# Placing the edges of a graph layer by matmuls with masks, and two equal chunks of edges

## The chip, the core and the metric

One core of a Trainium2 chip runs the kernel. Its engines are TensorE (PE, with its weight loads as PEld), VectorE (DVE), ScalarE (ACT), GpSimd (POOL) and SyncE (SP), each with its own stream of instructions, coupled by semaphores. The metric is the device time of one execution in microseconds; lower is better.

## What is computed

```python
xn = layernorm(x)                       # x: 6250 x 256
agg = segment_sum(xn[nbr], dst_of_edge) # 100000 edges
mean = agg / max(count, 1)
x = x + xn @ W1.T + b1 + mean @ W2.T + b2 + mix(xn)   # mix: 8 heads of key-value products, plus xn
x = x + experts(layernorm(x))           # top-1 of 8 experts, capacity 977
```

The edges' source ids aren't sorted by the node they are summed into, so the kernel sorts them itself. It brings every edge into a slot of a "tile" of 128 slots, in which all edges belong to one block of 128 nodes (49 blocks).

## The kernel before

Five stages follow one another.

**1. Table, counts and places of chunk 0.** The edges lie as 125 partitions by 800 columns, and two chunks of columns are sorted apart: 352 columns and then 448 (`chunk_plan`, L51). For the layernorm and the table of `xn` times W2 in two float16 parts, eight blocks at a time go through VectorE (`pair`, L753), ScalarE (`normal`, `turned`, `high`), TensorE (`turn`, `table`, L515 to L536) and out by GpSimd's queue. Between these, VectorE finds each edge's place. `count` (L879) makes a mask of "edge is of block b" for each of 49 blocks and counts it by an accumulator; `place` (L815 on VectorE, L546 on TensorE) turns the counts into the place where each block begins on each partition; and `rank` (L898) makes the mask again, runs a prefix sum over it (the scan, L911) and copies the sums under the mask into `pos` (L918). One turn of the loop at L921 is `rank` for 7 blocks and then one `pair`.

**2. Sort of chunk 0.** For each column of edges VectorE writes one-hots of the slot in its tile (`LH`, L945; every third column a scaled one too, L952) and of the tile (`HT`, L956). ScalarE scales them (`LV`, L479), and two matmuls (L566) add the edge's two numbers into banks `psV`. `decode` (L863) makes `idx` and `srcl` of them. The gathers wait for it.

**3. Tiles of chunk 0.** GpSimd issues one indirect gather of 128 rows per tile (L398) into a ring of 32; TensorE multiplies it with a one-hot of its nodes (L586, L587); VectorE adds the result to the block (L804). Between tiles, VectorE does all of `second_chunk` (L962), that is counts, places and sort of chunk 1, split over the tiles by `side_plan` (L85), which has a cost for each step and must be done 32 tiles before the chunk's end; `columns_by` tells TensorE which columns to multiply behind which tile.

**4. Tiles of chunk 1.** Between the tiles the head products (`heads`, one per group of 16 tiles) and then each block's own product with W1 (`own`, one block per 4 tiles, L636 on TensorE and L1091 on VectorE).

**5. Nodes and experts** (`nodes`, `experts`), which the change doesn't touch.

Chunk 0 has 400 tiles (`T0`), chunk 1 has 496: the count is an upper bound on what any graph needs, rounded up to 16. The tiles that no edge fills gather one and the same row 128 times.

Of the kernel before, what the change touches and what calls it, by code (L numbers as in the profile page):

```python
# [5 lines left out]
ALU = mybir.AluOpType  # L6
# [10 lines left out]
P = 128  # L17
# [62 lines left out]
HEAD0, KV_AT = 1, 1 + NB // HD + 1  # L80
OWN0 = KV_AT
assert len(CHUNKS) == 2 and OWN0 + NB // LD + 1 <= CHUNKS[1][3] // GR and NB % LD == 1 and COLS1 % LB == 0


def side_plan():  # L85
# [16 lines left out]
    return done, place, sort, decode  # L102


SIDE, PLACE, SORT, DECODE = side_plan()
PLACE_AT = next(t for t in range(T0) if SIDE[t] > PLACE)
DECODE_AT = next(t for t in range(T0) if SIDE[t] > DECODE)

# [95 lines left out]
def edges(nc, ctx, kk, dram, x, src, dst, w1t, w2t, gb1, gb2, kw, kb, vw, vb, gate_w, gate_b):  # L204
# [5 lines left out]
    def sem(name):  # L210
# [26 lines left out]
    b7 = sb("b7", [P, B7], F32)  # L237
    n7 = sb("n7", [P, B7], F32)
# [21 lines left out]
    cnt = sb("cnt", [P, NB], F32)  # L260
    mi = sb("mi", [P, 2 * NB], I32)
    mrow = sb("mrow", [P, NB], F32)
    mend = sb("mend", [P, NB], F32)
    base = sb("base", [P, NB], F32)
# [34 lines left out]
    s_cnt, s_pre, s_mc, s_ec, s_ge, s_bk = (sem(n) for n in (  # L299
        "bucket_counts", "bucket_prefix", "tile_counts", "tile_ends", "tiles_past_ends", "tile_buckets"))  # L300
# [21 lines left out]
    block = ctx.enter_context(nc.Block())  # L322

# [183 lines left out]
    def _(pe):  # L507
# [30 lines left out]
        def table_of(i):  # L538

            turn(4 * i, 8 * i, 2)  # L540
            for g in range(4 * i, 4 * i + 4):
                if g < 4 * i + 3:
                    turn(g + 1, 2 * g + 2, 2)
                table(g, 2)

        def place(c, pp, pq):  # L546
            tiles = CHUNKS[c][3]
            pe.wait_ge(s_cnt, c + 1)

# [44 lines left out]
        table_of(0)  # L594
        place(0, psP, psQ)
        n = NB // (2 * LD)
        for i in range(1, n):
            table_of(i)
# [56 lines left out]
        for t in range(T0, TILES):  # L655
            g, s = (t - T0) // GR, (t - T0) % GR
            if g == KV_AT and s == 0:
# [11 lines left out]
            if HEAD0 <= g < KV_AT and s >= 10:  # L669
                m, pieces = g - HEAD0, (HD if g - HEAD0 < NB // HD else 1) * 2  # L670
                if s == 10:
                    pe.wait_ge(s_kn, m + 1)
                products(m, range(min(s - 10, pieces), min(s - 9, pieces)), pieces - 1)
            if OWN0 <= g and s % 2 == 0 and (g - OWN0) * LD + s // 4 < NB:
                own((g - OWN0) * LD + s // 4, s % 4)

    @block.vector
    def _(v):
# [17 lines left out]
        v.tensor_copy(iota_b[:, :], iota_i[:, 0:NB])  # L696
        v.tensor_copy(XA[:, RW - 1:NB * RW:RW], mi[:, 0:NB])
# [852 lines left out]
```

## Time and profile before

| what | us |
|---|---|
| median of 3 runs (2236.62 to 2239.11) | 2238.36 |
| the profiled execution | 2236.5 |
| its span | 2234.9 |

| engine | busy us | share |
|---|---|---|
| PE | 1573.9 | 70% |
| DVE | 1518.3 | 68% |
| POOL | 1056.0 | 47% |
| ACT | 721.1 | 32% |

A share over the whole span mixes five stages with different limits, so it tells little here. The stages are to be read apart, from the busy times of stretches and from the moments at which the work of one stage lets the next begin. In a row of the timeline, the first number is the start, the second the duration; the bracket at the end tells how long the engine sat idle before and what it waited for. PEclk is the granted TensorE clock, as a share of 2.4 GHz.

### The profile page before, as it was taken

To read this page: it belongs to the slowest core of one execution; us is meant where nothing else is said; L and a number is where in the kernel's file an instruction comes from. 1 tells how busy PE (TensorE), PEld (TensorE's weight loads), DVE (VectorE), ACT (ScalarE), POOL (GpSimd) and SP (SyncE) were. 2 spreads that over 40 slices of the span, in tenths; PEclk is the share of its full clock that TensorE was granted. 3 is DMA by queue.
4 is the path that set the end of the run, shared out by engine and by line. 5 is a ranking of instruction groups with operands and counts; after the bars stand their busy time and mean duration, and the time that the engine had idled before them with its cause. 6 is when DMAs were issued, how large, how long until landed. Compare 5 with 4: busy or idle time off the path is not lost. (4 is left out here: it accounts for less than half of the span.)

```text
span 2234.9 us, 27232 instructions
## 1 busy us (share of the span) xinstructions
PE 1573.9 (70%) x6303; PEld 838.9 (38%) x6303; DVE 1518.3 (68%) x4295; ACT 721.1 (32%) x2020; POOL 1056.0 (47%) x1037
## 2 busy tenths in 40 slices
PE   2363887444477777766565557888747499999997
PEld 2351332110022222223222224444436266666665
DVE  8978999899988888877665656555457144444444
ACT  1243998000077777720000001111036122222221
POOL 2001000777777766667777777777705311111111
PEclk8677999555599999975555556766555599999999
DMA  4117000333333322463333334444745512222310
GB/s 141 38 57 299 12 0 0 97 92 90 90 99 104 97 81 78 79 99 98 104 106 101 103 104 130 127 126 121 94 110 202 163 48 87 94 92 95 96 49 5
DMA packets 89940, 212.70 MB, mean 95 GB/s; under 512 B 20882, under 2 KB 50104, under 8 KB 86848
## 3 DMA queue, kind: packets, MB, share of 16 engines
q0 software_dynamic: 52656, 140.17, 23.9%
q1 hardware_dynamic: 35496, 70.56, 9.4%
q8 instruction: 50, 0.82, 0.2%
q10 hardware_dynamic: 1680, 0.67, 0.1%
q14 instruction: 58, 0.48, 0.1%
HBM read 166.08 MB, written 49.89 MB: 97 GB/s over the span
## 5 line engine op out<-in xcount | busy, mean ns | idle before, releaser
L398 POOL DMA_INDIRECT G<-xn_parts,idx x448 | 455.0, 1016 | 339.6 <-DVE srcl L876 165.1
L804 DVE TENSOR_TENSOR XA<-XA,bank 128x257 f32 x896 | 375.3, 419 | 333.6 <-PE bank L587 302.0
L479 ACT ACTIVATE LV<-LH,v 125x128 f16<-125x128 f16 x1490 | 449.5, 387 | 340.4 <-DVE LH L1003 309.3
L398 POOL DMA_INDIRECT w<-xn_parts,idx x448 | 459.2, 1025 | 136.5 <-issue 136.5
L566 PE MATMUL bank<-HT,LV 125*128 125x496 f16 (+1 forms) x1600 | 401.4, 359 | 141.9 <-ACT LV L479 66.8
L586 PE MATMUL bank<-G,S 128*128 128x257 f16 x448 | 159.1, 355 | 199.2 <-DMA G<-xn_parts,idx 166.5
L1520 POOL DMA_INDIRECT out<-ob,tok x64 | 66.7, 1042 | 402.3 <-DVE ob L1506 399.6
L586 PE MATMUL bank<-w,S 128*128 128x257 f16 x448 | 158.8, 355 | 135.1 <-DMA w<-xn_parts,idx 118.7
L566 PEld LDWEIGHTS bank<-HT,LV 125*128 125x128 f16 x1600 | 117.6, 98 | 361.4 <-ACT LV L479 187.1
L1444 PE MATMUL bank<-w,ht 128*117 128x256 f32 (+1 forms) x1024 | 223.7, 379 | 0.0
L1433 PE MATMUL bank<-xt,w 128*128 128x468 f32 (+1 forms) x512 | 215.6, 580 | 0.8 <-ACT xt L1458 0.8
L1444 PEld LDWEIGHTS bank<-w,ht 128*117 128x117 f32 (+1 forms) x1024 | 188.8, 186 | 30.5 <-issue 0.4
L1468 ACT ACTIVATE ht<-bank,b1c 128x468 f32<-128x468 f32 (+1 forms) x128 | 85.7, 669 | 334.1 <-PE bank L1433 334.1
L1497 DVE TENSOR_TENSOR y<-bank,b 128x256 f32<-128x256 f32 (+1 forms) x64 | 27.2, 424 | 235.2 <-PE bank L1444 235.2
L586 PEld LDWEIGHTS bank<-G,S 128*128 128x128 f16 x448 | 47.3, 106 | 330.0 <-DMA G<-xn_parts,idx 270.4
L587 PE MATMUL bank<-G,S 128*128 128x256 f16 x448 | 164.8, 368 | 0.0
L587 PE MATMUL bank<-w,S 128*128 128x256 f16 x448 | 164.3, 367 | 0.0
L586 PEld LDWEIGHTS bank<-w,S 128*128 128x128 f16 x448 | 47.0, 105 | 274.7 <-DMA w<-xn_parts,idx 220.5
L1008 DVE TENSOR_SCALAR HT<-iota_t,tf 125x496 f16<-125x496 f16 x448 | 149.5, 362 | 0.0
L1433 PEld LDWEIGHTS bank<-xt,w 128*128 128x128 f32 x512 | 98.1, 192 | 109.6 <-issue 107.1
L784 DVE TENSOR_TENSOR S<-iota,srcl 128x1024 f16<-128x1024 f16 x112 | 136.6, 1220 | 2.3 <-issue 2.2
L489 ACT ACTIVATE work<-work 128x768 f32<-128x768 f32 (+1 forms) x17 | 13.9, 818 | 315.8 <-DVE work L1039 315.8
(223 smaller groups left out, 2073.9 us busy)
## 6 DMA issues: line engine op xcount, KB each, us to landing
w<-f SPq DMA_DIRECT2D x16, 1024.0 KB, 7.4
expert_rows<-G SPq DMA_DIRECT2D x7, 2048.0 KB, 19.4
xb<-expert_rows SPq DMA_DIRECT2D x8, 1028.0 KB, 11.9
xb<-expert_rows SPq DMA_DIRECT2D x8, 939.7 KB
G<-xn_parts,idx POOLq DMA_INDIRECT x448, 2.8
w<-xn_parts,idx POOLq DMA_INDIRECT x448, 2.8
XA<-x SPq DMA_DIRECT2D x6, 1024.0 KB, 5.6
xn_parts<-G POOLq DMA_DIRECT2D x12, 512.0 KB, 3.7
```

What stands on the lines that cost most here:

```text
L398: pool.indirect_dma_start(g[:, o:o + 2 * D], None, tab, bass.IndirectOffsetOnAxis(ap=idx[:, t:t + 1], axis=0)).then_inc(s_g[t % RING], 16)
L479: ins = act.activation(LV[0:EP, (2 * q + n) * P:(2 * q + n + 1) * P], LH[0:EP, q * P:(q + 1) * P], ACT.Copy, scale=v[0:EP, ds(col, 1)])
L566: ins = pe.matmul(psV[n][:, 0:tiles], LV[0:EP, (2 * q + n) * P:(2 * q + n + 1) * P], HT[0:EP, q * TMAX:q * TMAX + tiles], start=False, sto ...
L586: pe.matmul(psA[t % AR][:, 0:AGW], lhs, g[:, o + D:o + 2 * D + 1], start=True, stop=True)
L587: pe.matmul(psA[t % AR][:, 0:D], lhs, g[:, o:o + D], start=False, stop=True, skip_group_check=True).then_inc(s_tile, 1)
L784: v.tensor_tensor(S[:, t % SR * P:(t % SR + SB) * P].rearrange("p (j n) -> p j n", n=P), iota_1[:, :].unsqueeze(1).to_broadcast([P, SB, P] ...
L804: v.tensor_tensor(XA[:, ds(o, AGW)], XA[:, ds(o, AGW)], psA[t % AR][:, 0:AGW], ALU.add).then_inc(s_ev, 1)
L1008: v.tensor_scalar(HT[0:EP, (q + j) * TMAX:(q + j) * TMAX + tiles], iota_t[0:EP, 0:tiles], tf[0:EP, k + j:k + j + 1], None, ALU.is_equal).t ...
L1433: ins = pe.matmul(psH[f % 2][:, 0:cols], w1[q][:, k * F + f * P:k * F + (f + 1) * P], xt[n % 2][:, k * TQ * P:k * TQ * P + cols], start=(k ...
L1444: ins = pe.matmul(psY[m % 2][0:rp, 0:D], ht[:, f * TQ * P + m * rp:f * TQ * P + (m + 1) * rp], w2[q][:, f * D:(f + 1) * D], start=(f == 0) ...
L1468: act.activation(ht[:, f * TQ * P:f * TQ * P + cols], psH[f % 2][:, 0:cols], ACT.Relu, bias=b1c[:, e * FT + f:e * FT + f + 1]).then_inc(s_ ...
L1520: pool.indirect_dma_start(out, bass.IndirectOffsetOnAxis(ap=tok[0:rp, s:s + 1], axis=0), ob[0:rp, s * D:(s + 1) * D], None, bounds_check=N ...
```

## The change

- Chunks of 400 and 400 columns; tiles are rounded up to 8, so 440 and 440 (880 in all instead of 896).
- `count` goes: VectorE only makes the mask (L888 of the changed kernel, no accumulator). TensorE multiplies each mask with a one-hot pattern `to_row` (L576), which adds, in one bank, the number of edges of block b in every column, in row b and once more in row 64 + b.
- `place` makes one scan over the 400 columns of that bank (L895 of the changed kernel) and from it the places at which each column of each block begins, as two bfloat16 parts in `begin16`.
- `rank` has no scan: two matmuls per block, mask times a triangle (`before`) and `of_row` times `begin16` (L597, L598), give the places in a bank, and VectorE copies them under the mask (L935). In chunk 0 two banks take turns (`psP`, `psQ`), in chunk 1 four.
- Chunk 0's counts are 25 and 24 behind the first two `pair`s, its ranks 12, 12, 12 and 13 behind the other four, and TensorE does them between its table matmuls. The loops are written out.
- In stage 3 the planner has lower costs for counts and ranks. In stage 4 a head product takes 12 tiles (`HS`) and a block's own product 3 (`OS`).

```diff
-    for cols in (352, 448):
+    for cols in (400, 400):
         tiles = (cols * EP + NB * (P - 1)) // P
-        tiles = -(-tiles // GR) * GR
+        tiles = -(-tiles // SB) * SB
...
+HS, OS = 12, 3
+HEAD0 = GR
+KV_AT = HEAD0 + HS * (NB // HD + 1)
...
+COUNTS = (25, 24)
+RANKS = (12, 12, 12, 13)
...
-    split = rank + NB + 2
+    split = rank + NB + RB1
-    costs = [800] * NB + [9000] + [2300] * (NB + 2) + [700] * 5 + ([1070] + [350] * (LB - 1)) * (COLS1 // LB) + [3000]
+    costs = [430] * NB + [8000] + [1100] * (NB + RB1) + [700] * 5 + ([1070] + [350] * (LB - 1)) * (COLS1 // LB) + [3000]
...
+        def counted(c, b, pp):
+            cols = CHUNKS[c][1]
+            m = 2 * c * NB + b
+            pe.wait_ge(s_mk, m + 1)
+            pe.matmul(pp[0:SROWS, 0:cols], to_row[0:EP, NB - 1 - b:NB - 1 - b + SROWS], masked(c, m), start=(b == 0),
+                      stop=(b == NB - 1)).then_inc(s_mu, 1)
...
+        def ranked(c, b, ring):
+            cols = CHUNKS[c][1]
+            m = (2 * c + 1) * NB + b
...
+            pe.wait_ge(s_mk, m + 1)
+            if b >= len(ring):
+                pe.wait_ge(s_cp, c * NB + b - len(ring) + 1)
+            out = ring[b % len(ring)][0:EP, 0:cols]
+            pe.matmul(out, before[0:EP, 0:EP], masked(c, m), start=True, stop=False)
+            pe.matmul(out, of_row[0:SROWS, b:b + 1].to_broadcast([SROWS, EP]), begin16[0:SROWS, 0:cols],
+                      start=False, stop=True).then_inc(s_mu, 1)
...
+        def mask_of(c, m, b):
+            c0, cols = CHUNKS[c][0:2]
+            if m >= B7:
+                v.wait_ge(s_mu, m - B7 + 1)
+            v.tensor_scalar(masked(c, m), blk[0:EP, c0:c0 + cols], iota_b[0:EP, b:b + 1], None,
+                            ALU.is_equal).then_inc(s_mk, 1)
...
+        def rank(c, r, ring):
...
+                mask_of(c, m, r)
+            if r >= n:
+                b = r - n
+                v.wait_ge(s_mu, m - n + 1)
+                if b:
+                    v.wait_ge(s_cp, c * NB + b)
+                v.copy_predicated(pos[0:EP, 0:cols], masked(c, m - n).bitcast(U16),
+                                  ring[b % n][0:EP, 0:cols]).then_inc(s_cp, 1)
...
-        with v.Fori(0, NB // B7) as i:
-            step_count.loop(i, 3)
-            count(i)
...
+        for i in range(PAIRS):
+            if i:
+                pair(i, True)
+            if i < len(COUNTS):
+                for b in range(sum(COUNTS[:i]), sum(COUNTS[:i + 1])):
+                    mask_of(0, b, b)
...
+                    place(0, psP, psQ)
+            else:
+                j = i - len(COUNTS)
+                for r in range(sum(RANKS[:j]), sum(RANKS[:j + 1])):
+                    rank(0, r, (psP, psQ))
```

How this moves instructions at two places:

TensorE, table phase, one group of eight blocks before (L524 transposes the normalized rows, L534 multiplies them with W2):

```order
L524 MATMUL bank<-ident,XA 128x128 x8
L534 MATMUL bank<-W,LV 128x256 x4
L524 MATMUL bank<-ident,XA 128x128 x4
L534 MATMUL bank<-W,LV 128x256 x4
L524 MATMUL bank<-ident,XA 128x128 x4
L534 MATMUL bank<-W,LV 128x256 x8
```

The begin of such a group after the change, in the part with ranks (L547 and L557 are the old L524 and L534):

```order
L547 MATMUL bank<-ident,XA 128x128 x4
L597 MATMUL bank<-mask,before 125x400
L598 MATMUL bank<-cum,of_row 125x400
L597 MATMUL bank<-mask,before 125x400
L598 MATMUL bank<-cum,of_row 125x400
L547 MATMUL bank<-ident,XA 128x128 x4
L557 MATMUL bank<-W,LV 128x256 x4
```

Two or three ranks have come between every two table products, so each is held up by masks and copies of VectorE, and the copies by the table.

TensorE, tiles of chunk 1, the blocks' own products before (L643 transposes, L649 and L651 multiply with W1 and add the bias, L586 and L587 are a tile):

```order
L643 MATMUL bank<-ident,work 128x128 x2
L586 MATMUL bank<-w,S 128x257
L587 MATMUL bank<-w,S 128x256
L586 MATMUL bank<-G,S 128x257
L587 MATMUL bank<-G,S 128x256
L649 MATMUL bank<-W,work 128x256 x2
L651 MATMUL bank<-brow,ones 128x256
```

And after the change (L703, L709, L711 and L628, L629 are the same lines):

```order
L703 MATMUL bank<-ident,work 128x128 x2
L628 MATMUL bank<-w,S 128x257
L629 MATMUL bank<-w,S 128x256
L709 MATMUL bank<-W,work 128x256 x2
L711 MATMUL bank<-brow,ones 128x256
```

One tile instead of two lies between a block's transposes and its products, and three instead of four between one block and the next.

## Rows read from the trace of the kernel before

**Rows 1.** Busy time by stretches: microseconds, and in brackets instructions, of each engine.
```profile
core 0: us, PE busy (x) PEld busy (x) DVE busy (x) ACT busy (x) POOL busy (x), PEclk, DMA share, GB/s
70.00:204.00 134.00, 60.75 (x248) 49.22 (x248) 110.84 (x281) 48.11 (x94) 13.46 (x15) 0.70 0.27 103
204.00:391.00 187.00, 150.40 (x706) 55.55 (x706) 178.25 (x889) 175.94 (x594) 0.17 (x1) 0.98 0.11 47
391.00:442.00 51.00, 21.70 (x72) 4.80 (x72) 47.41 (x137) 0.00 (x0) 39.13 (x38) 0.51 0.33 95
470.00:611.00 141.00, 57.88 (x192) 12.70 (x192) 132.19 (x248) 0.00 (x0) 111.75 (x97) 0.50 0.31 90
650.00:750.00 100.00, 77.47 (x371) 28.91 (x370) 85.49 (x225) 76.47 (x252) 76.23 (x79) 1.00 0.36 103
800.00:900.00 100.00, 77.83 (x376) 29.35 (x375) 84.02 (x224) 76.98 (x253) 62.39 (x60) 1.00 0.28 80
1000.00:1300.00 300.00, 178.84 (x668) 80.67 (x668) 192.35 (x387) 15.98 (x30) 229.30 (x233) 0.52 0.36 102
1400.00:1500.00 100.00, 84.16 (x315) 47.47 (x313) 55.16 (x127) 13.24 (x39) 76.23 (x79) 0.72 0.44 129
1590.00:1617.00 27.00, 19.61 (x60) 10.16 (x58) 11.81 (x26) 2.45 (x7) 20.30 (x23) 0.50 0.90 84
```

**Rows 2.** Timeline: GpSimd's first gathers of both chunks, last gather, last tile's add.
```profile
391.59 1.03 POOL L398 DMA_INDIRECT G<-xn_parts,idx  x1 [164.13 <-DVE srcl L876]
...
974.93 0.95 POOL L398 DMA_INDIRECT G<-xn_parts,idx  x1 [0.96 <-DVE srcl L876]
...
1616.83 0.95 POOL L398 DMA_INDIRECT w<-xn_parts,idx  x1 [0.30 <-issue]
...
1637.10 0.42 DVE L804 TENSOR_TENSOR XA<-XA,bank 128x257 f32 x1 [0.20 <-DVE XA L804]
```

**Rows 3.** Groups by line: name, count, then busy us and mean ns of one.
```profile
L911 DVE TENSOR_TENSOR_SCAN cum<-onesw,n,mask 125x352 f32<-125x352 bf16 x49 | 45.4, 938 | 0.2
...
L918 DVE COPY_PREDICATED pos<-mask,cum 125x352 f32<-125x352 uint16 x49 | 26.0, 531 | 1.0
...
L956 DVE TENSOR_SCALAR HT<-iota_t,here 125x400 f16<-125x400 f16 x352 | 96.4, 314 | 0.0
...
L1008 DVE TENSOR_SCALAR HT<-iota_t,tf 125x496 f16<-125x496 f16 x448 | 149.5, 362 | 0.0
```

**Rows 4.** Timeline, one group of eight blocks in the table phase, and the next one's begin.
```profile
103.77 1.97 PE L524 MATMUL bank<-ident,XA 128*128 128x128 f32 x8 [6.22 <-ACT XA L424]
...
111.84 3.62 PE L534 MATMUL bank<-W,LV 128*128 128x256 f32 x16
...
113.65 1.40 DVE L722 BATCH_NORM_STATS2 lnst<-XA 128x6 f32 x4
...
122.44 1.97 PE L524 MATMUL bank<-ident,XA 128*128 128x128 f32 x8 [6.98 <-ACT XA L424]
```

**Rows 5.** Timeline, VectorE: counts' begin and end, first ranks, and the last step before the sort.
```profile
28.94 0.17 DVE L880 COPY b<-iota_b 125x7 f32 x1
...
59.60 0.06 DVE L811 MEMSET mcol<- 128x4 f32 x1
...
65.34 1.64 DVE L904 TENSOR_SCALAR mask<-blk,b 125x352 bf16<-125x352 bf16 x7
...
204.38 0.34 DVE L859 CAST pos<-cum 125x352 f32<-125x352 int32 x1
```

**Rows 6.** Timeline, VectorE: two turns of the sort loop over 16 columns.
```profile
303.59 0.17 DVE L936 COPY here<-pos 125x16 f32 x1
...
311.77 0.17 DVE L936 COPY here<-pos 125x16 f32 x1
```

**Rows 7.** Timeline, tile stage: one gather on GpSimd, one mask on VectorE.
```profile
600.62 0.95 POOL L398 DMA_INDIRECT w<-xn_parts,idx  x1 [0.30 <-issue]
600.95 0.33 DVE L987 TENSOR_SCALAR mask<-blk,iota_b 125x448 bf16<-125x448 bf16 x1
```

More of the change, by code:

```diff
@@ L101, in side_plan, with side_by @@
     assert done[-1] == len(costs)
-    return done, place, sort, decode
-SIDE, PLACE, SORT, DECODE = side_plan()
+    assert all(b - a < RB1 for a, b in zip(done, done[1:]) if rank <= a < split)
+    return done, place, rank, sort, decode
+SIDE, PLACE, RANK, SORT, DECODE = side_plan()
 PLACE_AT = next(t for t in range(T0) if SIDE[t] > PLACE)
 DECODE_AT = next(t for t in range(T0) if SIDE[t] > DECODE)
+def side_by(t, first, n):
+    return n if t >= T0 else min(max(SIDE[t] - first, 0), n) if t >= 0 else 0
 def columns_by(t):
@@ L259, in edges @@
     tli = cum[:, WMAX:2 * WMAX].bitcast(I32)
[L260 to L264, printed above, removed]
+    mi = sb("mi", [P, NB], I32)
+    to_row = sb("to_row", [P, SROWS + NB - 1], BF16)
+    of_row = sb("of_row", [P, NB], BF16)
+    before = sb("before", [P, P], BF16)
+    ends = sb("ends", [P, SROWS], F16)
+    mc16 = sb("mc16", [P, 2], F16)
+    begins = cum[:, 0:WMAX]
+    summed = cum[:, WMAX:2 * WMAX]
+    begin16 = cum[:, 2 * WMAX:2 * WMAX + WMAX // 2].bitcast(BF16)
     mcol = sb("mcol", [P, 4], F32)
@@ L593, in _, with first_chunk @@
         ins.then_inc(s_w2n, 1)
[L594 to L598, printed above, removed]
+        def first_chunk(i, part):
+            if i < len(COUNTS):
+                b0, n = sum(COUNTS[:i]), COUNTS[i]
+                for b in range(b0 + n * part // 4, b0 + n * min(part + 1, 4) // 4):
+                    counted(0, b, psP)
+                if i == len(COUNTS) - 1 and part == 4:
+                    place(0, psQ)
+            else:
+                b0, n = sum(RANKS[:i - len(COUNTS)]), RANKS[i - len(COUNTS)]
+                for b in range(b0 + n * part // 5, b0 + n * (part + 1) // 5):
+                    ranked(0, b, (psP, psQ))
+        n = PAIRS
+        for i in range(n):
+            table_of(i, lambda part: first_chunk(i, part))
         turn(4 * n, NB - 1, 1)
@@ L696, in _ @@
         v.tensor_copy(iota_b[:, :], iota_i[:, 0:NB])
+        v.tensor_copy(before[:, :], upper[:, :])
+        v.tensor_copy(of_row[0:64, :], ident[0:64, 0:NB])
+        v.tensor_copy(of_row[64:SROWS, :], ident[64:SROWS, 64:SROWS])
+        v.tensor_copy(ends[0:NB, 0:64], upinc[0:NB, 0:64])
+        v.tensor_copy(ends[0:NB, 64:SROWS], upinc[0:NB, 0:NB])
+        step(v.memset(to_row[:, :], 0.0))
+        wait()
+        v.memset(to_row[:, NB - 1:NB], 1.0)
+        v.memset(to_row[:, 64 + NB - 1:64 + NB], 1.0)
         v.tensor_copy(XA[:, RW - 1:NB * RW:RW], mi[:, 0:NB])
@@ L840, in place @@
+            wait()
+            v.tensor_tensor(begin16[64:R, 0:cols], begins[64:R, 0:cols], begin16[64:R, 0:cols],
+                            ALU.subtract).then_inc(s_bg, 1)
             v.wait_ge(s_bk, c + 1)
@@ L877, in decode @@
             v.wait_ge(s_dec, c + 1)
-        def count(i):
-            step(v.tensor_copy(b7[0:EP, :], iota_b[0:EP, ds(i * B7, B7)]))
-            wait()
-            for j in range(B7):
-                o = j * WMAX
-                ins = v.tensor_scalar(mask[0:EP, o:o + COLS0], blk[0:EP, 0:COLS0], b7[0:EP, j:j + 1], 0.0,
-                                      ALU.is_equal, ALU.add, accum_out=n7[0:EP, j:j + 1])
-            step(ins)
-            wait()
-            step(v.tensor_copy(cnt[0:EP, ds(i * B7, B7)], n7[0:EP, :]))
@@ L926, in _ @@
+        for r in range(NB, NB + RB0):
+            rank(0, r, (psP, psQ))
         last()
-        with v.Fori(0, NB // B7 - first) as i:
-            step_count.loop(i, 2 + 2 * B7)
-            rank(i + first)
-        step_count.end(NB // B7 - first)
+        v.wait_ge(s_cp, NB)
         for _ in split(COLS0, pos):
```

186 lines of the change are left out of this document (76 added, 110 removed).

## Prediction

> **What bounds the kernel now.** I read the stretches first [rows 1], since the shares over the whole span mix five stages. Table and places (70 to 204): VectorE busy 110.84 of 134 us, TensorE 60.75. Sort of chunk 0 (204 to 391): VectorE 178.25 and ScalarE 175.94 of 187, and meanwhile GpSimd waits 164.13 us for the sorted indices [rows 2]. Tiles of chunk 0: up to 611 GpSimd issues gathers without a pause (a gather's mean is 111.75 / 97 = 1.15 us, and 0.30 us lie between two, as the last gather's bracket shows [rows 2]); from 611 on VectorE's sort of chunk 1 sets the pace, since 800 to 900 holds only 60 gathers where 650 to 750 held 79, the ring of 32 being full by then. Tiles of chunk 1: GpSimd again, 233 gathers of 0.98 us in 300 us, so 1.29 us per tile, while VectorE is busy 64% and TensorE 60%. The moments [rows 2] give the lengths: 391.59 to 974.93 is 583.3 us for 400 tiles (1.458 each), 974.93 to 1616.83 is 641.9 us for 495 steps (1.297 each), and the last tile is added 20.3 us after the last gather. This lag is read in 1590 to 1617: DMA share 0.90 at 84 GB/s, against 0.36 at 102 GB/s from 1000 to 1300. Those are the tiles that no edge fills, which read one row over and over.
>
> So the sum has five terms. Nodes and experts have the same instructions before and after: nothing.
>
> **Term 1, table and places.** Removed on VectorE: 49 scans (45.4 us) and the accumulating form of the count. The copies stay (26.0 us for 352 columns [rows 3], about 29 for 400). Removing some 65 us of work is not a gain of 65, as TensorE now stands between mask and copy, in its own order with the table. The chain per group of eight blocks is what counts. Today TensorE takes from 103.77 to 115.46, 11.7 us, and from VectorE's statistics (113.65) to TensorE's next transposes (122.44) it is 8.8 us [rows 4]. After the change both lie on one chain: VectorE can leave a group only after TensorE's tenth of 12 ranks (two banks), and that comes behind the last table product. A matmul of 400 columns costs 150.40 / 706 = 0.21 us at PEclk 0.98 [rows 1], so a rank is 0.43 us there and at most 0.85 at the half clock. A group with ranks: 8.8 + 11.7 + 10 x 0.43 = 25 us, at most 29 with the half clock; with hand-overs I take 26, against 18.7 today (103.77 to 122.44) with its ranks inside VectorE.
> Laid out: masks begin at 28.94 [rows 5]. Group 0 with 25 counts: 11.7 us and 25 x 0.21 to 0.43, ends near 48; the next normalization takes 5 of the 8.8 us, as the statistics are done by then; group 1 ends near 73. `place` took 5.7 us (59.60 to 65.34 [rows 5]) and gets two or three operations over 400 columns: VectorE is free at 79, TensorE starts group 2 at 88, group 5 at 88 + 3 x 26 = 166, and is through at 183; two last copies, the last block and five small steps make 10. The sort starts at about 193 instead of 204.4: **-12 us**. Bounds: -22 (groups of 25 and counts at full clock, 3 us less overlap loss) and +5 (groups of 29).
>
> **Term 2, sort of chunk 0.** 16 columns take 8.18 us [rows 6]. Columns go from 352 to 400, and `HT` from 400 to 440 wide. From 400 to 496 wide its mean rose from 314 to 362 ns at most [rows 3], partly by the neighbours, so 40 more are 10 to 20 ns: 8.18 + 16 x 0.01 = 8.35 us. 25 x 8.35 - 22 x 8.18 = **+29 us** (up to +32).
>
> **Term 3, tiles of chunk 0.** 440 instead of 400, and chunk 1's side work falls: no scans (49 over 448 columns, each above the 0.94 us of 352 columns [rows 3]), 400 columns for 448, and they spread over 283 tiles instead of 213, 1.41 columns per tile for 2.10. Today a tile with 2.10 columns takes 100 / 60 = 1.67 us. Taking 0.5 us for VectorE's part without columns leaves 0.55 per column, so 1.41 columns make 1.28 us. GpSimd's pace is 76.23 / 79 + 0.30 = 1.26 (650 to 750) or 1.29 (1000 to 1300): the stage becomes one of gathers. The ring lets VectorE fall back 32 tiles, so it may take (283 x 1.30 + 32 x 1.30) / 283 = 1.45 us per tile free of charge. What is issued: 38 tiles with counts at 39.13 / 38 + 0.30 = 1.33; 83 with ranks between 1.28 and today's 1.45, I take 1.38; 319 at 1.30. Sum 51 + 114 + 415 = 580 us against 583.3: **-3 us**, with bounds -14 (all at 1.29 after the counts) and +25.
> Gather and VectorE: one gather of 0.95 us, as short as they get, has a mask of 0.33 us inside it [rows 7], so I charge masks nothing. The Trainium skill (SBUF — State Buffer, "Who interferes with whom") states that `tensor_scalar` shuts GpSimd out when it runs in a two-port mode, but not in the form that writes an accumulator; that speaks against this change, which turns 49 counts from the latter form into the former. By that rule stage 3 would get up to 49 x 0.33 = 16 us longer (an estimate by that page). The row doesn't agree.
>
> **Term 4, tiles of chunk 1.** 440 x 1.297 = 571 against 641.9: **-71 us**. This is the term that carries the sum. It is hidden nowhere: the gathers follow one another here. It needs the consumers to keep up with blocks every 3 tiles. TensorE: 178.84 / 233 = 0.77 us per tile at PEclk 0.52, 84.16 / 79 = 1.07 with blocks at 0.72. Brought to 0.72 the tile is 0.56, so a block is 4 x (1.07 - 0.56) = 2.0, and with 3 tiles per block 0.56 + 0.67 = 1.23 us per tile, just under 1.30. Bounds: -74 and -45 (rival B).
>
> **Term 5, the lag at the end.** Unfilled tiles: edges fill on average 400 x 125 / 128 + 49 / 2 = 415 of 440, so 25 instead of 496 - 462 = 34. The lag of 20.3 us is 5 of ordinary lag and 15 gathered over these: 15 x 25 / 34 = 11. **-4 us**. The same 25 in chunk 0 arrive late too, but into a full ring, with nothing to be delayed but tiles that catch up.
>
> **Sum.** -12 + 29 - 3 - 71 - 4 = -61. The profiled execution took 2236.5 us (span 2234.9), 1.9 under the median of 2238.36. 2236.5 - 61 = 2175.5, beside the median 2177. I forecast **2176 us**.
>
> **Rivals.**
> *A. TensorE and VectorE wait for each other in the table phase.* Only two banks are in turn, and a table product stops the copies. If each of the four parts of a group loses 1.5 us, a group takes 32 instead of 26: 4 x 6 = +24, **2200**. For it: PEclk is 0.70 there, so the half clock is often granted. Against: more matmuls fall into the gaps in which it waits for ScalarE today. 15%.
> *B. The blocks' own products don't keep up.* With PEclk 0.52 a block is 2.8 us, a tile then 0.77 + 0.93 = 1.70; over 147 tiles 59 us fall behind, 41 are in the ring, and the rest costs about 20: **2196**. Against: 73 tiles without blocks follow, and a busier TensorE has had a higher clock (0.72 at 84% busy, 0.52 at 60% [rows 1]). 8%.
> *C. Gathers get quicker where the scans go, and the groups take 25 or less.* 83 x 0.09 + 319 x 0.02 = 14, and 8 in term 1: **2154**. 11%.
> *D. The gathers of stage 3 stay at 1.45 throughout*, because copies and onehots on VectorE stand in GpSimd's way and the split brings nothing there: 440 x 1.45 = 638, +58: **2234**, no change. 3%.
> *E. Slower: in the tiles with columns TensorE drops to the half clock.* Today it is 1.00 there at 78% busy, 77.83 / 60 = 1.30 us per tile. With 1.41 columns, 440 wide: a tile alone 0.39 (half of 0.77), a column (1.30 - 0.39) / 2.10 = 0.43, times 0.89 for the width, so 0.39 + 1.41 x 0.38 = 0.93 of 1.30 us, 72% busy, but at the half clock 1.86 us per tile. 283 x 1.86 = 526 for 368, less 42 of the ring: +116, **2292**. It is slower than today from 1.66 us per tile on. For it: in the stretch with 60% busy the clock was 0.52. Against: 72% lies nearer to 78, and at the half clock it would be busy all the time, where rows 1 shows the higher clock with more work. 5%. The Trainium skill (TensorE: Matmul & The Clock Gate, Part 1) states that the slow clock is the default and activity lifts it. By that rule E heals itself; the trace agrees as far as the busier stretches have the higher clock.
>
> **Chances and range.** Forecast 58%, A 15, B 8, C 11, D 3, E 5. The range 2145 to 2208 holds the forecast's own bounds (mainly terms 1 and 3), A, B and C, and leaves out D, E and the ends where two of the costs meet. A measurement tells about 0.2% (4.5 us) from no change. Faster 0.93, same 0.02 (D at its middle), slower 0.05 (E).
>
> **What would show it.** First gather at 405 to 412 instead of 391.59 (terms 1 and 2: sort begins near 193, 8.35 us per 16 columns). First gather of chunk 1 some 580 us later, waiting for a sort that is long done rather than for TensorE's ring. GpSimd without waits but 0.30 from there to its last gather 571 us later. PEclk near 1 in the tiles with columns and above 0.72 in those with own blocks. The forecast is wrong if stretches of stage 3 or 4 hold fewer than 75 gathers per 100 us, or if the sort starts after 205.

## The result, and the profile of the changed kernel

The change takes **2170.66 us** (median of 4 runs, 2167.32 to 2174.5) against 2238.74 for the kernel before (4 runs of the same comparison): ratio 0.9697 with an interval of 0.9675 to 0.972, so 68 us less. The forecast was 2176 us, 61 less, with a range of 2145 to 2208. The sign, the time and the range held. Of the five terms the first lay outside its bounds, the second half a microsecond over its upper one, and the prediction's view of TensorE's clock in stage 4 was wrong. The profiled execution took 2167.32 us (span 2165.4).

Stretches of the changed kernel, columns as in [rows 1]:

```profile
core 0: us, PE busy (x) PEld busy (x) DVE busy (x) ACT busy (x) POOL busy (x), PEclk, DMA share, GB/s
70.00:176.00 106.00, 64.22 (x298) 50.29 (x298) 66.59 (x198) 40.09 (x75) 8.10 (x11) 0.81 0.15 51
176.00:395.00 219.00, 179.31 (x802) 63.09 (x802) 209.15 (x1007) 200.03 (x675) 3.83 (x3) 0.98 0.18 74
400.00:500.00 100.00, 71.01 (x252) 31.43 (x251) 73.13 (x192) 0.00 (x0) 76.23 (x79) 0.60 0.36 103
650.00:750.00 100.00, 65.12 (x354) 29.26 (x354) 80.50 (x213) 63.66 (x210) 77.44 (x75) 0.98 0.35 98
800.00:900.00 100.00, 64.45 (x348) 29.12 (x349) 79.61 (x211) 61.43 (x202) 77.34 (x75) 0.98 0.34 98
1000.00:1300.00 300.00, 173.66 (x709) 87.55 (x708) 196.02 (x413) 21.53 (x45) 230.50 (x229) 0.60 0.36 103
```

The first row shows what the change took from VectorE: 66.59 us where it had 110.84 in 134 [rows 1]. The rows 650 to 750 and 800 to 900 are alike now, 75 gathers each, where there were 79 and 60: the stage has no part left in which VectorE sets the pace.

The moments, in the timeline (they answer to [rows 2, 4, 5]):

```profile
29.72 0.32 DVE L888 TENSOR_SCALAR mask<-blk,iota_b 125x400 bf16<-125x400 bf16 x1
...
62.35 0.99 DVE L895 TENSOR_TENSOR_SCAN cum<-onesw,bank 113x400 f32<-113x400 bf16 x1 [2.76 <-PE bank L576]
...
67.15 1.41 DVE L794 BATCH_NORM_STATS2 lnst<-XA 128x6 f32<-128x256 f32 x4
...
100.08 1.11 PE L547 MATMUL bank<-ident,XA 128*128 128x128 f32 x4 [8.01 <-ACT XA L447]
...
114.81 0.60 DVE L935 COPY_PREDICATED pos<-mask,bank 125x400 f32<-125x400 uint16 x1 [0.89 <-PE bank L598]
115.31 1.39 DVE L794 BATCH_NORM_STATS2 lnst<-XA 128x6 f32<-128x256 f32 x4
...
124.09 1.11 PE L547 MATMUL bank<-ident,XA 128*128 128x128 f32 x4 [8.01 <-ACT XA L447]
...
176.01 0.17 DVE L996 COPY here<-pos 125x16 f32 x1 [0.32 <-DVE pos L952]
176.14 3.53 DVE L997 COPY here<-v 125x16 f32 x1
...
395.05 1.03 POOL L421 DMA_INDIRECT G<-xn_parts,idx  x1 [173.25 <-DVE srcl L969]
...
981.59 0.94 POOL L421 DMA_INDIRECT G<-xn_parts,idx  x1 [0.30 <-issue]
...
1555.62 0.95 POOL L421 DMA_INDIRECT w<-xn_parts,idx  x1 [0.30 <-issue]
...
1569.49 0.42 DVE L877 TENSOR_TENSOR XA<-XA,bank 128x257 f32 x1 [0.85 <-PE bank L629]
```

Subtract them stage by stage. A row "tiles" is the time from the chunk's first gather to the next chunk's first, or to the last gather.

| us | before | change | difference | forecast |
|---|---|---|---|---|
| up to the sort of chunk 0 | 205.05 | 176.01 | -29.0 | -12 |
| sort of chunk 0 | 186.5 | 219.0 | +32.5 | +29 |
| tiles of chunk 0 | 583.3 | 586.5 | +3.2 | -3 |
| tiles of chunk 1 | 641.9 | 574.0 | -67.9 | -71 |
| last gather to last tile | 20.3 | 13.9 | -6.4 | -4 |
| nodes and experts, to the end | 597.8 | 595.9 | -1.9 | 0 |
| span | 2234.9 | 2165.4 | -69.5 | -61 |

The largest gain stands in stage 4, and the longer sort of chunk 0 takes half of it back. A table of differences between two kernels does not yet say which part of the change earned it: the change moves columns from the one chunk to the other, and it makes places cheaper in both. The experiments take these apart.

### The profile page after: what moved, and what is told of

Its sections match the earlier page's. It is cut to its first block and busy times, and to the rows that moved or that the text cites. A ratio compares the mean times of both kernels' runs of the same rounds, so it can differ in the third digit from the quotient of the medians.

```text
span 2165.4 us, 27487 instructions
## 1 busy us (share of the span) xinstructions
PE 1564.5 (72%) x6551; PEld 872.1 (40%) x6551; DVE 1393.2 (64%) x4116; ACT 717.9 (33%) x2005; POOL 1035.4 (48%) x1021
## 5 line engine op out<-in xcount | busy, mean ns | idle before, releaser
L877 DVE TENSOR_TENSOR XA<-XA,bank 128x257 f32 x880 | 369.3, 420 | 367.4 <-PE bank L629 344.0
L421 POOL DMA_INDIRECT G<-xn_parts,idx x440 | 445.7, 1013 | 307.1 <-DVE srcl L969 173.2
L608 PE MATMUL bank<-HT,LV 125*128 125x440 f16 x1600 | 385.0, 357 | 177.8 <-ACT LV L502 98.5
L421 POOL DMA_INDIRECT w<-xn_parts,idx x440 | 447.9, 1018 | 134.1 <-issue 134.1
L628 PE MATMUL bank<-G,S 128*128 128x257 f16 x440 | 149.5, 340 | 133.2 <-DMA G<-xn_parts,idx 104.9
L628 PE MATMUL bank<-w,S 128*128 128x257 f16 x440 | 149.9, 341 | 99.7 <-DMA w<-xn_parts,idx 88.7
L629 PE MATMUL bank<-w,S 128*128 128x256 f16 x440 | 152.8, 347 | 0.0
L629 PE MATMUL bank<-G,S 128*128 128x256 f16 x440 | 152.3, 346 | 0.0
L628 PEld LDWEIGHTS bank<-G,S 128*128 128x128 f16 x440 | 47.4, 108 | 234.8 <-DMA G<-xn_parts,idx 164.4
L1045 DVE TENSOR_SCALAR HT<-iota_t,tf 125x440 f16<-125x440 f16 x400 | 130.2, 348 | 0.0
L628 PEld LDWEIGHTS bank<-w,S 128*128 128x128 f16 x440 | 47.8, 109 | 198.1 <-DMA w<-xn_parts,idx 154.7
L1016 DVE TENSOR_SCALAR HT<-iota_t,here 125x440 f16<-125x440 f16 x400 | 114.2, 327 | 0.0
```

The source lines that it names most:

```text
L421: pool.indirect_dma_start(g[:, o:o + 2 * D], None, tab, bass.IndirectOffsetOnAxis(ap=idx[:, t:t + 1], axis=0)).then_inc(s_g[t % RING], 16)
L608: ins = pe.matmul(psV[n][:, 0:tiles], LV[0:EP, (2 * q + n) * P:(2 * q + n + 1) * P], HT[0:EP, q * TMAX:q * TMAX + tiles], start=False, sto ...
L628: pe.matmul(psA[t % AR][:, 0:AGW], lhs, g[:, o + D:o + 2 * D + 1], start=True, stop=True)
L629: pe.matmul(psA[t % AR][:, 0:D], lhs, g[:, o:o + D], start=False, stop=True, skip_group_check=True).then_inc(s_tile, 1)
L877: v.tensor_tensor(XA[:, ds(o, AGW)], XA[:, ds(o, AGW)], psA[t % AR][:, 0:AGW], ALU.add).then_inc(s_ev, 1)
L1016: v.tensor_scalar(HT[0:EP, q * TMAX:q * TMAX + tiles], iota_t[0:EP, 0:tiles], tfh[0:EP, n:n + 1], None, ALU.is_equal).then_inc(s_ht, 1)
```

## The experiments

Twelve kernels were timed, four on each of three chips, each four beside the kernel before; one kernel is among them twice. The first of the second four is the change itself, unaltered: 0.970 was expected of it on a chip like that of the result, and it came to 0.9721. Beside the first result its profile also tells what the same kernel varies by: 3.5 us in the tiles of chunk 1 (577.5 and 574.0) and 1.9 us in the lag at the end (12.0 and 13.9). The same moments of the second and third four, all in us:

| kernel | sort begins | first gather | first of chunk 1 | last gather | last tile | median | ratio (95%) |
|---|---|---|---|---|---|---|---|
| change again | 176.4 | 395.4 | 981.7 | 1559.2 | 1571.2 | 2170.1 | 0.9721 (0.9705 to 0.9737) |
| ranks alone | 192.7 | 408.9 | 996.6 | 1578.1 | 1590.2 | 2183.57 | 0.9777 (0.9761 to 0.9793) |
| spread | 179.8 | 399.9 | 986.3 | 1557.1 | 1560.7 | 2160.09 | 0.9673 (0.9657 to 0.9689) |
| 336 and 464, spread | 173.6 | 354.9 | 886.2 | 1542.4 | 1545.9 | 2146.58 | 0.9618 (0.9602 to 0.9634) |
| 368 and 432, spread | 177.1 | 377.7 | 927.2 | 1541.2 | 1544.8 | 2141.12 | 0.9592 (0.9574 to 0.961) |
| masks accumulate | 180.3 | 399.0 | 985.8 | 1561.7 | 1573.8 | 2169.1 | 0.9715 (0.9696 to 0.9735) |
| own 72 later | 177.8 | 397.7 | 981.9 | 1555.3 | 1576.1 | 2170.78 | 0.9717 (0.9697 to 0.9738) |
| even split, scans | 215.6 | 431.5 | 1033.2 | 1611.6 | 1623.1 | 2221.15 | 0.9952 (0.9935 to 0.9968) |

The kernel before took 2231.55 us (7 runs) beside the second four (the first four rows), 2232.6 (7 runs) beside the third.

### The first four: a chip on which every kernel is slower

Four kernels: the change with 352 and 448 columns, with 336 and 464, and with a block's own product every 4 tiles; and the kernel before with the even split.

```diff
-    for cols in (400, 400):
+    for cols in (352, 448):
```


> The change with its first chunk back at 352 columns and the second at 448 (392 and 488 tiles, 880 in all as in the change). Theory 'gathers set both tile stages': the unhidden sort falls by 3 x 16 columns at 8.6 us, -27 us with the narrower masks; 392 tiles at 1.33 us make 522 (586 in the change), 488 at 1.31 make 638 (574 in the change): these two cancel, total about 2141 us. Rival 'the even split pays': 448 columns at the 0.80 us of the kernel before are 358 us behind some 110 tiles of counts and ranks, the sort of chunk 1 sets the pace of stage 3, which takes 560 us or more, and the total is 2170 or above.

```diff
-    for cols in (400, 400):
+    for cols in (336, 464):
```


> The same with 336 and 464 columns (376 and 504 tiles). Gathers set the pace: another -9 us against the run with 352, about 2132. If 464 columns over 249 tiles (1.86 per tile) are more than the ring can hide (0.5 + 1.86 x 0.55 = 1.52 us per tile against 1.33 + 0.17 of the ring), it gives back 5 to 15 us and equals the run with 352; then 352 is the optimum.

```diff
-HS, OS = 12, 3
+HS, OS = 12, 4
```


> The change with a block's own product every 4 tiles again instead of 3, nothing else. Theory 'the backlog is hidden by the ring and by the tiles behind it': VectorE's lag behind the gathers stays below 10 us where the change shows 23, and the time is the same within 5 us. Rival 'TensorE at half clock delays the stage': 5 to 20 us faster. Should the profile show PEclk 0.50 with TensorE over 95% busy here too, the clock doesn't follow the load in this stage.

To the kernel before:
```diff
-    for cols in (352, 448):
+    for cols in (400, 400):
...
-        tiles = -(-tiles // GR) * GR
+        tiles = -(-tiles // SB) * SB
...
+HS, OS = 12, 3
+HEAD0 = GR
+KV_AT = HEAD0 + HS * (NB // HD + 1)
```


> The kernel before with the even split (400 and 400 columns, 440 and 440 tiles) and the 12 and 3 tile steps of stage 4, but places by VectorE's scans as before. Theory: sort +32, stage 4 -68, end -6, stage 1 +6 (49 scans and copies over 400 columns); stage 3 has 440 tiles with VectorE's scans, between 583 (400 columns instead of 448 pay for 40 tiles) and 640 (gathers at 1.45): total 2200 to 2260, I take 2215. So places by TensorE would be worth about 45 of the 68 us. Rival 'the split makes the gain': 2185 or less.

(The second of them also makes the buffer `cum` 5 * WMAX // 2 columns wide instead of 3 * WMAX.) Measured, against 2371.03 us for the kernel before on this chip (13 runs), in this order: 2322.62 (ratio 0.9786, 0.9751 to 0.982), 2307.87 (0.9748, 0.9718 to 0.9777), 2339.9 (0.987, 0.9847 to 0.9893) and 2375.31 (1.0028, 1.001 to 1.0045). The kernel before is 132 to 139 us slower here than in the other comparisons. In the third kernel, from 1100 to 1200, some waits (what waited for what: us in total, times, longest) are

```profile
PEld bank L628 <- issue: 73.5, 46, 6.2
...
DVE XA L877 <- remote: 29.3, 8, 8.4
```

and in the changed kernel, on the chip of the result, TensorE's weight loads of that line wait for landing gathers:

```profile
PEld bank L628 <- DMA G<-xn_parts,idx: 36.4, 32, 1.8
...
PEld bank L628 <- DMA w<-xn_parts,idx: 33.4, 31, 1.9
```

TensorE and VectorE stand still for up to 6 and 8 us with nothing that the profile shows to wait for. Stops of 3.3 to 9.4 us each between 413 and 462 put the tiles from 8 to 46 us behind their gathers, which fills the ring, and a tile costs 1.50 us on average in the third kernel ((1719.3 - 397.6) / 879, by its first and last gather). What stops the engines stayed open; the other comparisons don't show it. So these four tell nothing on the gathers' pace, and what the third was to tell of the half clock (blocks every 4 tiles) isn't told. They do show that the first gather moves by the sort, 397.6, 364.9 and 354.9 us for 400, 352 and 336 columns, and that the even split without the rest is no gain. The first is also the only run of the masks with the old split: 48 us less than the kernel before, on this chip. The fourth was run again on another chip.

### What the split alone brings

> The kernel before with the columns divided evenly, tiles rounded to 8 and the shorter steps of stage 4 only: VectorE keeps its accumulating counts and its scans. On the first chip of the experiments it was no faster than before (1.0028), but there all tiles took 1.5 us. Theory (the split pays only because the scans left stage 3): first gather 391.6 + 39 = 431 as on that chip; stage 3 has room for the scans only partly: 440 tiles at 1.29 to 1.47 (before had 1.458), about 615; stage 4 571; lag 14; in all some 6 us under before, ratio 0.997, while the change has 0.970 to 0.972. Rival (the split alone carries the gain of stage 4, as the prediction's largest term has it, and stage 3 does not care): stage 3 takes 586 as in the change: ratio 0.985.

The same kernel as the fourth above. **Measured 0.9952: 11 us, of the 61 that the change has in such a comparison.** The rival (0.985) falls, and the direction of the theory stands; stage 3 took 601.7 us, not 615. Its first gathers of both chunks and its last:

```profile
431.47 1.03 POOL L400 DMA_INDIRECT G<-xn_parts,idx  x1 [195.71 <-DVE srcl L882]
...
1033.18 0.94 POOL L400 DMA_INDIRECT G<-xn_parts,idx  x1 [1.25 <-PE bank L589]
...
1611.57 0.95 POOL L400 DMA_INDIRECT w<-xn_parts,idx  x1 [0.30 <-issue]
```

Against the kernel before: first gather +39.9, stage 3 +18.4, stage 4 -63.5, lag -8.7, end -1.4, together -15 of the profiled spans (which come from two chips). The split moves work, and nearly all that stage 4 wins is paid back in the places, the sort and stage 3. Against this kernel the change has its first gather 36 us earlier, and stage 3 is 15 us shorter (586.3, change again): this is what the masks on TensorE bring, with the planner's costs that go with them. The largest term of the forecast was the right number in the right stage, but it was not what made the change pay.

### Ranks within the groups, or alone

```diff
-            else:
-                b0, n = sum(RANKS[:i - len(COUNTS)]), RANKS[i - len(COUNTS)]
-                for b in range(b0 + n * part // 5, b0 + n * (part + 1) // 5):
-                    ranked(0, b, (psP, psQ))
...
         table(4 * n, 1)
+        for b in range(NB):
+            ranked(0, b, (psP, psQ))
```
(and the same order on VectorE, behind `last`)

> All 49 ranks of chunk 0 behind the last block's table instead of 12, 12, 12 and 13 within the last four groups. Theory (a group took 24.0 us with its ranks, TensorE and VectorE fill each other's gaps): a group without ranks takes 18 to 19, 4 x 5.5 = 22 us less, the ranks alone are bound by VectorE at mask 0.33 + copy 0.60 + hand-over, 49 x 1.0 = 49 us, so the sort starts some 27 us later than in the change. Rival (in the groups both engines wait for each other, as the prediction's one chain has it): the groups with ranks cost as much as both apart, and the sort starts within 8 us of the change.

Measured 13.5 us slower than the change again, the sort 16.3 later: between the two. VectorE's last statistics come at 122.6 instead of 165.9, but TensorE's table ends only at 141.5, and the first rank starts at 145.5:

```profile
135.00:192.00 57.00, 44.63 (x118) 17.25 (x116) 46.00 (x110) 3.02 (x6) 6.07 (x6) 0.58 0.74 305
```

The 49 ranks end at 190.3, 45 us later. In the change they end at 166, so being within the groups saves 24 us, near to the 27 expected. What I had left out is the other end. In the change the last block's table and five small steps take 10 us from 166 to 176, with VectorE waiting 3.3 us for ScalarE (4.3 in the kernel with spread gathers). Here only the small steps follow the ranks, 2.3 us. That gives 8 back. A version with some ranks kept for behind the last block should get both; it wasn't tried.

### Gathers of unfilled tiles, spread over rows

```diff
+        v.tensor_scalar(own_row[:, :], mi[:, 0:1], 32.0, None, ALU.mult)
...
+            step(v.tensor_scalar(d, a, 0.0, own_row[:, 0:1], ALU.is_equal, ALU.mult))
+            wait()
+            step(v.tensor_tensor(idx[:, ch0:ch0 + tiles], idx[:, ch0:ch0 + tiles], d, ALU.add))
```


> Only the gathers of unfilled tiles changed: each partition reads its own row instead of all one row. Theory (one row read 128 times makes the gathers land late): the last tile comes 5 us after the last gather instead of 14, and the mean DMA share of the last 30 us falls from 0.9 to under 0.5; two operations more in each decode cost 1 us each, one of them on the path: 7 to 8 us faster than the change. Rival (the lag is own products that TensorE still owes): the lag stays at 14 and the time within 2 us.

Measured 10.0 us faster than the change again. The last 15 us before the last tile, change again:

```profile
1556.00:1571.00 15.00, 5.60 (x19) 1.19 (x18) 3.82 (x9) 0.00 (x0) 3.23 (x4) 0.50 0.83 70
```

and with spread gathers:

```profile
1546.00:1561.00 15.00, 7.31 (x24) 1.58 (x24) 6.03 (x13) 0.00 (x0) 9.26 (x10) 0.50 0.32 96
```

The DMA share falls from 0.83 to 0.32 while more is moved (96 GB/s for 70), and 13 tiles are added for 9. The last tile comes 3.6 us after the last gather, not 12.0. So one row read 128 times by a gather is what made the lag, as term 5 had it; the rival falls. The two operations on the path take 1.1 us. The lag explains 8.4 of the 10 us. The rest is no gain of the padding that the trace shows: the sort begins 3.4 us later here (179.8 and 176.4) and the gathers of stage 4 take 6.8 us less (570.7 and 577.5), spread over the whole stage.

### How many columns for chunk 0, once places are cheap

> Columns 336 and 464 instead of 400 and 400, and the gathers of unfilled tiles spread over 128 different rows. Theory (the sort of chunk 0 costs 8.76 us per 16 columns, and stage 3 has room, as the gathers set its pace): the sort falls by 4 x 8.7 = 35 us, the tiles stay 880 at their pace, the end lag falls by 8: 43 us below the change, less up to 10 where TensorE and VectorE now fill the ring in stage 3. Rival (the even split is what made stage 3 a stage of gathers): with 464 columns over some 240 tiles, 1.9 per tile, VectorE needs 1.6 us per tile, stage 3 grows by 240 x 0.3 less 40 of ring = 30 us, and the split gains nothing: within 10 us of the change.

This is the spread kernel with 336 and 464 columns. Measured 2146.58 us, 13.5 under the spread kernel with equal halves. Neither theory's number: the first gather comes 45 us earlier as expected, but first to last gather is 1187.5 us instead of 1157.2, so 30 of it is given back, the rival's price. From 720 to 820 the sort of chunk 1 sets the pace again:

```profile
720.00:820.00 100.00, 74.73 (x367) 29.29 (x365) 83.90 (x221) 73.08 (x240) 63.73 (x65) 1.00 0.29 84
```

65 gathers, and GpSimd's waits there are

```profile
POOL G L422 <- PE bank L630: 25.0, 27, 1.8
```

that is 25 us in which GpSimd waits for TensorE to free a slot of the ring, 8 of them the 0.30 us that lies between any two gathers. The add of a tile came at most 55 us after the start of its gather in stage 3, 25 us with equal halves. Hence the size between, which should fill the ring and hardly more:

```diff
-    for cols in (336, 464):
+    for cols in (368, 432):
```


> Columns 368 and 432 with the spread gathers of unfilled tiles. With 336 and 464 the ring was full in stage 3 (gathers 1.56 to 1.60 us apart for 128 tiles, 531 us for 376 tiles where 1.333 each would be 501), so 30 of the 45 us that the shorter sort gained were given back; with 400 and 400 VectorE was 19 us behind at most, of some 42 that the ring holds. Theory (the ring's slack may be used up, but not more): first gather at 377, 1.69 columns per tile, the ring just fills near the end, first to last gather about 1165: 2140 us, 6 under 336 and 464, 20 under the split in halves with spread gathers. Rival (ring-full time grows from 400 on in proportion to the columns moved): first to last gather 1172, 2147, the same as with 336 and 464.

Measured 2141.12, and first to last gather 1163.5: the theory's 2140 and 1165, not the rival's 2147 and 1172. Tiles are up to 51 us behind their gathers. From 780 to 880 GpSimd issues 73 gathers of 1.05 us:

```profile
780.00:880.00 100.00, 68.00 (x356) 28.99 (x355) 80.34 (x212) 67.29 (x221) 76.94 (x73) 1.00 0.33 96
```

Its waits for the ring, from 780 to 880 and from 880 to 930:

```profile
POOL G L422 <- PE bank L630: 2.7, 6, 0.7
...
POOL G L422 <- PE bank L630: 8.4, 10, 2.3
```

So the ring is full near the end of the chunk, and costs little. This is the fastest kernel of the study, ratio 0.9592, 29 us under the change (2170.1 and 2141.12, from two chips on which the kernel before agrees within 1.1 us); 10 of them go to the spread gathers. Equal halves aren't the best split once places are cheap: of the three sizes tried, 336 costs 5 us more (the two intervals just overlap) and 400 costs 19. The first four point the same way, in spite of their stops: 0.9748 and 0.9786 with 336 and 352 columns, 0.987 with 400 and blocks every 4 tiles. The old 352 lies between the two better sizes, so nothing here shows that the even split earns anything within the change; 352 with masks wasn't run on a chip like that of the result.

### Masks with an accumulator

```diff
-            v.tensor_scalar(masked(c, m), blk[0:EP, c0:c0 + cols], iota_b[0:EP, b:b + 1], None,
-                            ALU.is_equal).then_inc(s_mk, 1)
+                v.tensor_scalar(masked(c, m), blk[0:EP, c0:c0 + cols], iota_b[0:EP, b:b + 1], 0.0, ALU.is_equal,
+                                ALU.add, accum_out=unread[0:EP, b:b + 1]).then_inc(s_mk, 1)
```


> The 49 masks of chunk 1's counts in the form that also writes an accumulator (which nothing reads). Theory (the plain form costs GpSimd nothing: the change has gathers 1.30 and 1.28 us apart over the first 64 tiles, the kernel before 1.35 with the accumulating form): the first 64 tiles do not get quicker, within 2 us; the time within 4 us of the change, ratio 0.969 to 0.973. Rival (the plain form shuts GpSimd out of SBUF for its 0.33 us): with accumulators the first 38 tiles take up to 49 x 0.33 = 16 us less, ratio 0.965 or below.

Groups by line while chunk 1 is counted; first with accumulators, then as changed (busy us, mean ns of one):

```profile
L890 DVE TENSOR_SCALAR_CACHE_REDUCE mask<-blk,iota_b 125x400 bf16<-125x400 bf16 x49 | 29.0, 623 | 0.0
...
L890 DVE DVE_READ_ACCUMULATOR mask<-blk,iota_b 125x1 f32 x49 | 4.0, 82 | 0.0
```

```profile
L888 DVE TENSOR_SCALAR mask<-blk,iota_b 125x400 bf16<-125x400 bf16 x49 | 14.3, 328 | 0.0
```

The mask takes twice as long and the gathers are no faster: 1.33 us apart over the first 32 tiles, 1.29 in the change again, and 1.31 against 1.28 over the next. The ratio is 0.9715, beside the 0.9721 of the change. The rival, which the Trainium skill states (SBUF — State Buffer, "Who interferes with whom": plain `tensor_scalar` can shut GpSimd out, the accumulating form can't), would have up to 16 us less. No run shows that for a gather.

### The blocks' own products 72 tiles later

```diff
-OWN0 = KV_AT
+OWN0 = KV_AT + 72
```


> The blocks' own products begin 72 tiles later, so that 24 plain tiles follow them instead of 96. Theory (TensorE's half clock belongs to this stretch of work: own products at 1.70 us per tile when it is granted; the ring of 32 and the plain tiles behind hide it): a stretch of some 60 us at PEclk 0.50 comes again, some 94 us later, in which the lag rises to about 20 us; the plain tiles left take back 24 x 0.5 = 12 of it, and the unfilled tiles add their own: last tile 18 to 24 us after the last gather instead of 12 to 14, so 5 to 10 us slower than the change. Rival (the half clock is bound to the moment, not to the work): it stands at 1380 to 1440 as before, now over the first own products, and the end is as in the change, within 2 us.

Changed kernel (half clock from 1380 to 1440) and this one (from 1480 to 1540):

```profile
1380.00:1400.00 20.00, 19.82 (x56) 11.06 (x55) 10.02 (x22) 2.75 (x8) 15.37 (x16) 0.50 0.45 125
1400.00:1420.00 20.00, 19.82 (x56) 11.03 (x53) 8.94 (x21) 2.76 (x8) 15.43 (x16) 0.50 0.45 127
1420.00:1440.00 20.00, 19.82 (x57) 11.30 (x56) 10.02 (x22) 2.75 (x8) 15.43 (x16) 0.50 0.43 129
1440.00:1460.00 20.00, 18.89 (x81) 11.22 (x79) 12.22 (x28) 3.93 (x12) 15.12 (x17) 0.79 0.47 134
1460.00:1480.00 20.00, 17.22 (x88) 10.27 (x88) 15.06 (x36) 3.34 (x10) 15.43 (x16) 1.00 0.42 121
```

```profile
1420.00:1440.00 20.00, 15.08 (x76) 8.31 (x74) 13.16 (x29) 3.44 (x10) 15.13 (x17) 1.00 0.47 140
...
1480.00:1500.00 20.00, 19.82 (x57) 11.02 (x56) 8.82 (x20) 2.76 (x8) 15.43 (x16) 0.50 0.45 131
1500.00:1520.00 20.00, 19.82 (x57) 10.93 (x56) 8.76 (x21) 2.52 (x8) 15.43 (x16) 0.50 0.44 122
1520.00:1540.00 20.00, 19.86 (x56) 11.28 (x56) 9.30 (x22) 2.38 (x8) 15.13 (x17) 0.50 0.74 105
```

The stretch at the half clock, with TensorE busy 99%, moved with the work, so it isn't bound to the moment. Its length isn't set by the work alone, though. The kernel with the even split and scans has the same own products every 3 tiles, from 1342 to 1522. Its clock over that part is higher, and the longest time at the half clock is some 20 us:

```profile
1340.00:1520.00 180.00, 154.06 (x667) 89.58 (x667) 110.84 (x254) 32.76 (x96) 138.24 (x138) 0.86 0.47 137
1489.00:1509.00 20.00, 19.82 (x57) 11.02 (x56) 8.64 (x21) 2.75 (x8) 15.19 (x16) 0.50 0.44 126
```

The last tile came 20.8 us after the last gather (18 to 24 expected, 12.0 in the change again). That number was met by luck: the expectation has 24 plain tiles behind the own products, but here they take up tiles 292 to 438 of 0 to 439. One tile follows, where 73 follow in the change, and nothing was taken back. And the time stayed the same, 2170.78, where 5 to 10 us more were expected: the profiled span is 4.0 us longer, since the gathers of stage 4 took 573.4 us instead of 577.5, and the medians show nothing (runs from 2165.21 to 2174.28). That the tiles behind cover the half clock is shown by the lag; what it would cost without them isn't.

## Why the prediction was right, and where not

**Right by its own mechanism:** terms 2, 4 and 5 and the sign. Stage 4 is one gather per 1.308 us (574.0 over 439 steps; forecast 1.297), with no wait but 0.30. The lag came from the unfilled tiles, as the spread gathers show; fewer of them, less lag. Without it 3.6 us are left, not the 5 of term 5. The stage's length was right though its consumers weren't what I had worked out (below).

**Term 1, -29 instead of -12, outside its bound of -22.** Two steps were too dear. "Group 1 ends near 73, VectorE is free at 79, TensorE starts group 2 at 88": the counts had ended at 62.35 and the next statistics began at 67.15, 12 us sooner. The stretches of the changed kernel from the first mask to the scan:

```profile
29.00:41.00 12.00, 10.90 (x48) 8.73 (x49) 6.47 (x29) 3.45 (x8) 0.00 (x0) 1.00 0.55 174
41.00:62.30 21.30, 16.99 (x88) 13.92 (x87) 12.90 (x50) 10.56 (x20) 1.85 (x2) 0.92 0.31 101
```

TensorE is busy 27.9 of 33.3 us, at a granted clock of 1.00 and 0.92. The group with the last 24 counts, its begin and its end:

```profile
49.76 1.11 PE L547 MATMUL bank<-ident,XA 128*128 128x128 f32 x4 [4.31 <-ACT XA L447]
...
62.15 1.03 PE L557 MATMUL bank<-W,LV 128*128 128x256 f32 x4
```

That is 13.4 us, where I had the 11.7 us of a group's table and 24 counts of 0.21 to 0.43 us on top, 17 to 22 us. The 11.7 came from a stretch at 0.70 [rows 1, 4]. The kernel before also has a clock of 1.00 from 29 to 41, which I hadn't read, so in the first group the higher clock isn't the counts' doing; from 41 to 65 it has 0.56, with TensorE busy 2.2 of 24 us. How much of the 12 us is clock and how much is counts lying in waits of TensorE within a group wasn't tried. Second, a group with ranks takes 24.0 us (100.08 to 124.09), not 26: the sum of its parts was 25, and I rounded hand-overs up. Three groups, 6 us. 12 + 6 is 18, and the miss is 17.

**Term 2, +32.5 instead of +29, just over its bound of +32.** The turn of 16 columns was right: its copies stand at 280.12, 288.48 and 296.84, 8.36 us apart (8.35 forecast). The rest is one row that term 1 brought about: `here<-v` took 3.53 us instead of 0.17, while GpSimd wrote zeros to `G`.

```profile
176.13 3.51 POOL L410 MEMSET G<- 128x4096 f32 x1 [1.48 <-DMA xn_parts<-G]
```

Before the change that stood at 182.50, 22 us ahead of the sort, beside scans and predicated copies of VectorE that took their usual 0.94 and 0.53 us. A step that gets earlier meets others' work that it used to follow.

**Term 3, +3.2 instead of -3,** inside its bounds. Two misses cancel in part: tiles with counts and ranks cost 1.29, not 1.33 and 1.38 (9 us), and those behind them 1.35 on average, not 1.30 (16 us). For those I had taken the pace of a stretch with 2.10 columns per tile and no ring full (79 gathers in 100 us [rows 1]). With 1.41 columns there are 75. Gathers of 1.03 us instead of 0.96 make the difference; why they are longer with less beside them stayed open.

**Term 4's check of TensorE was wrong, without harm.** I had 1.23 us per tile with own products, at PEclk 0.72, and set rival B (1.70 us at the half clock) aside because "a busier TensorE has had a higher clock". It happened: three stretches of 20 us stand at PEclk 0.50 with 19.82 us busy and 56 or 57 matmuls, 5.09 us per block of 3 tiles, so 1.70 per tile, the rival's number. What kept the rival from its 20 us is that TensorE was at it for some 60 us and not for 147 tiles: 23 us behind at most, out of 41 that the ring holds, and the next 48 tiles took it back, at PEclk 0.79 and 1.00 at first. On average the part with own products (1280 to 1480) has 0.75, which is above the 0.72 that I had named as a sign, and hides this. The same rows speak against the sentence on rival E: the Trainium skill (TensorE: Matmul & The Clock Gate, Part 1) states that activity lifts the slow clock, and I let E heal itself by that. For 60 us activity didn't.

**Rivals.** A (groups of 32) and D (1.45 per tile throughout) didn't come about; C's groups did (24.0), C's gathers not; E didn't: PEclk is 0.98 in both stretches with columns. The mark of 75 gathers per 100 us held in the stretches shown, and only just: at 1.35 us per tile the part with columns comes to 74, so other stretches of 100 us hold 73 or 74. By its letter that sign of being wrong came about, for the stage's own miss of 6 us. The sort began before 205. The first gather came at 395, not at 405 to 412, by term 1.

**What the right sum hid.** I read -71 as the split's and the masks as the -12 and -3. By parts the split alone brings 11 us (0.9952), and the masks some 50, 36 up to the first gather and 15 in stage 3, which the split had lengthened by 18 as long as the scans were in it. The -29 and +3 of the table compare with scans over 352 columns, and so show too little of the masks: with the split alone the first gather comes 40 us later, with masks as well 3.5 us.

## What to carry to other kernels

Price a change of several parts not only by stage but also with each part alone: the part whose gain is seen in a stage may be paid for by another, and the best size (368 of the three tried) shows only when both are in place. With a ring between two stages, the best size here was the one that just fills it, and a late engine shows as lag long before it shows as time. Padding deserves a look for what it reads: unfilled tiles that read one row cost 8.4 us of lag.

## What was not expected of the hardware

- A gather of 128 times one row lands late: with 128 different rows the DMA share in the same stretch was 0.32 instead of 0.83, at 96 instead of 70 GB/s.
- TensorE stayed at the half clock for some 60 us while 99% busy, after stretches at 0.83 and 1.00, and this time varies between kernels with the same own products every 3 tiles: some 60 us in the change and with spread gathers, 40 in the change again, 20 with the even split and scans. With blocks every 4 tiles the kernel before had 0.72 at 84% busy [rows 1]. What decides it stayed open.
- A GpSimd memset of 3.51 us held up VectorE's short copies and a mask, 3.53 and 3.63 us for copies of 0.17, and 3.44 us for a mask of 0.33 (ranks alone), but not the scans and predicated copies beside it in the kernel before. Where copies and the mask are held, the trace agrees with the Trainium skill (SBUF — State Buffer, "Who interferes with whom"), which says that the one is blocked for the other's whole instruction.
- On the chip of the first four kernels the kernel before took 2371 us instead of 2232 to 2239, and the comparison of two kernels there isn't the one on another: 1.0028 and 0.9952 for the same pair.
